# When the rows of a batch are turned: two at a time over two PSUM banks, or all four in one go over four

## What is computed

```python
# layer 0, for every batch b (x: 32 x 512 x 512, adj: 512 x 512)
y = einsum('nm,bmd->bnd', adj, x)
z = einsum('bnd,do->bno', y, weight) + bias
u = layernorm(x + z)                    # per row
# layer 1: q, k, v = u @ w_qkv ; attn = softmax(where(adj == 0, -inf, q k^T / 8))
#          o = attn v @ w_proj + b_proj ; out = layernorm(u + o + (norm(o) * gamma + beta))
```

## Time and profile before

| what | value |
|---|---|
| median of 3 runs | 3647.48 us (3646.9 to 3648.03) |
| the profiled execution: its own time | 3647.64 us |
| its span | 3645.8 us |
| TensorE (PE) busy | 3579.6 us, 98% |
| VectorE (DVE) busy | 2764.4 us, 76% |
| ScalarE (ACT) busy | 2223.4 us, 61% |
| GpSimd (POOL) busy | 1863.8 us, 51% |
| 16 DMA engines, first layer | some 55 to 65% busy, 170 to 196 GB/s |
| a batch of the first layer | 23.69 us, and 32 of them end at 777.5 us |

### The profile page before, as it was taken

The page is one execution under the profiler, slowest core; times in us unless marked ns, Lnnn a source line. Parts: engine busy times, 40 slices in busy tenths (PEclk is TensorE's granted clock), DMA queues, the critical chain, the costliest instruction groups (busy, mean ns, idle before and its releaser), DMA issues.

```text
span 3645.8 us, 64651 instructions
## 1 busy us (share of the span) xinstructions
PE 3579.6 (98%) x18960; PEld 2872.5 (79%) x18960; DVE 2764.4 (76%) x6557; ACT 2223.4 (61%) x4629; POOL 1863.8 (51%) x2559
## 2 busy tenths in 40 slices
PE   8999999999999999999999999999999999999996
PEld 6888888877777777777777777777777777777775
DVE  7666666656778787888877778787777778787787
ACT  4444443436666666666666666666666666666664
POOL 4555555532545555555555555555555555455555
PEclk9999999999999999999999999999999999999998
DMA  6555555540111111111111111111111111111111
GB/s 196 184 184 175 170 173 176 180 141 24 56 55 51 46 46 49 46 46 46 49 46 46 46 49 46 46 46 46 46 46 47 58 48 46 46 46 46 46 54 36
DMA packets 344958, 276.19 MB, mean 76 GB/s; under 512 B 13664, under 2 KB 275808, under 8 KB 344928
## 3 DMA queue, kind: packets, MB, share of 16 engines
q1 hardware_dynamic: 344928, 275.83, 24.9%
HBM read 141.56 MB, written 134.22 MB: 76 GB/s over the span
## 4 chain that ended last, share of the span: by engine, by line
PE 82%; DVE 9%; ACT 4%; issue 3%; POOL 1%; SPq 0%; DMA 0%; ACTq 0%; DVEq 0%; POOLq 0%
PE bank L813 17%; PE bank L796 10%; PE bank L829 10%; PE bank L773 10%; PE bank L311 9%; PE bank L762 9%; PE bank L324 9%; PE bank L847 6%; DVE pt_lo L1010 2%; PE bank L333 1%; ACT probs L893 1%; DVE o_stats L1036 1%; DVE ot_lo L1032 1%; DVE o L1053 1%; DVE probs L996 1%
## 5 line engine op out<-in xcount | busy, mean ns | idle before, releaser
L893 ACT ACTIVATE probs<-probs,bias_row 128x512 f32<-128x512 f32 x1024 | 729.0, 713 | 488.9 <-DVE bias_row L996 488.9
L1010 DVE TENSOR_TENSOR pt_lo<-bank,pt_hi 128x512 fp32r<-128x512 f32 x1024 | 668.2, 684 | 95.1 <-ACT pt_hi L901 82.2
L695 POOL TENSOR_SCALAR probs<-probs,inv_sums 128x480 f32<-128x480 f32 (+1 forms) x1024 | 688.3, 685 | 0.0
L996 DVE CUSTOM_DVE_ANT_0 probs<-bank,mask_bias 128x512 f32<-128x512 f32 x1024 | 661.6, 684 | 0.0
L901 ACT ACTIVATE pt_hi<-bank 128x512 fp32r<-128x512 f32 x1024 | 554.9, 594 | 132.3 <-PE bank L773 129.2
L692 POOL TENSOR_TENSOR probs<-probs,inv_sums 128x32 f32<-128x32 f32 x512 | 123.8, 242 | 986.6 <-DVE inv_sums L1002 983.0
L773 PE MATMUL bank<-ident,probs 128*128 128x128 f32 x4096 | 533.9, 273 | 20.6 <-POOL probs L695 16.9
L773 PEld LDWEIGHTS bank<-ident,probs 128*128 128x128 f32 x4096 | 477.8, 140 | 90.4 <-POOL probs L695 24.6
L813 PE MATMUL bank<-x_hi,w_hi 128*128 128x512 f32 x1024 | 411.3, 402 | 16.5 <-DVE ot L1028 6.4
L813 PE MATMUL bank<-x_hi,w_lo 128*128 128x512 f32 x1024 | 412.2, 403 | 0.0
L813 PE MATMUL bank<-x_lo,w_hi 128*128 128x512 f32 x1024 | 401.3, 392 | 0.0
(11 more groups left out here) (92 smaller groups left out, 7965.3 us busy)
## 6 DMA issues: line engine op xcount, KB each, us to landing
x_in<-in_x_dram SPq DMA_DIRECT2D x32, 1024.0 KB, 5.7
ut_hi<-ut_hi_sb SPq DMA_DIRECT2D x128, 256.0 KB, 3.5
ut_lo<-ut_lo_sb SPq DMA_DIRECT2D x128, 256.0 KB, 3.7
u_beta_rows<-ub SPq DMA_DIRECT2D x32, 1024.0 KB, 4.4
x_hi<-ut_hi SPq DMA_DIRECT2D x128, 256.0 KB, 4.3
x_lo<-ut_lo SPq DMA_DIRECT2D x128, 256.0 KB, 4.7
out_dram<-o SPq DMA_DIRECT2D x128, 256.0 KB, 3.3
ub_row<-u_beta_rows SPq DMA_DIRECT2D x124, 256.0 KB, 2.7
```

What stands on the lines that cost most here:

```text
L695: pool.tensor_scalar(probs[:, k % 2, a, cols], probs[:, k % 2, a, cols], inv_sums[:, k % 4, a:a + 1], 0.0, ALU.mult, ALU.add)\
L893: act.activation(probs[:, k % 2, a, :], probs[:, k % 2, a, :], ACT.Exp, bias=bias_row[:, k % 4, a:a + 1], scale=-1.0, accum_out=sums[:, k ...
L996: dve.tensor_tensor_reduce(probs[:, k % 2, a, :], s_bank[k % 2][a][:], mask_bias[:, k % T, :], -SCALE, 3.0e38, ALU.add, ALU.min, bias_row[ ...
L1010: dve.tensor_tensor(pt_lo[:, a, :, cols], t_bank[a][:].rearrange("p (m n) -> p m n", m=T), f32(pt_hi[:, a, :, cols]), ALU.subtract).then_i ...
```

## The change

- The turned rows get four PSUM banks (4 to 7) in place of two; in the last batch still two (4 and 5), since the second layer starts in banks 6 and 7.
- TensorE turns all four row groups of batch b - 1 in one go, behind y(b, 1). `turn(b, j)` of the same batch, between and behind the z units, is gone. The last batch's rows 0 and 1 are turned behind the loop, ahead of the first q matmuls. Batch 1 stands written out ahead of TensorE's loop.
- ScalarE's and VectorE's four `ut` parts of batch b - 1 stand behind the second y part of batch b.
- SyncE's queue stores all four turned row groups of batch b - 1 behind the store of `ub` of b - 1.

```diff
-            turn_bank = psum[4:6]
+            def turn_bank(b, j):
+                return psum[4 + (j % 2 if isinstance(b, int) and b == B - 1 else j)]
...
                     if not first:
                         store_ub(b - 1)
-                        store_ut(b - 1, 2)
-                        store_ut(b - 1, 3)
+                        for j in range(T):
+                            store_ut(b - 1, j)
                     if isinstance(b, int) and b < 2:
                         more_w(4 + 8 * b)
                     if last:
...
                         load_u_turned(sp, 0)
-                    store_ut(b, 0)
-                    store_ut(b, 1)
                     if isinstance(b, int) and b == 0:
                         more_w(8)
...
-                def turn(b, j, free=True):
-                    pe.wait_ge(u_made, b * 4 + (j + 1))
-                    if free:
-                        pe.wait_ge(utlo_made, b * 4 + (j - 1))
-                    for d in range(T):
-                        last = pe.transpose(turn_bank[j % 2][:, d * P:(d + 1) * P], u[:, j, d * P:(d + 1) * P],
-                                            ident[:])
-                    last.then_inc(u_turned, 1)
+                def turn(b):
+                    for j in range(T):
+                        pe.wait_ge(u_made, b * 4 + (j + 1))
+                        if not (isinstance(b, int) and b == 0):
+                            pe.wait_ge(utlo_made, b * 4 + (j - 3))
+                        for d in range(T):
+                            last = pe.transpose(turn_bank(b, j)[:, d * P:(d + 1) * P],
+                                                u[:, j, d * P:(d + 1) * P], ident[:])
+                        last.then_inc(u_turned, 1)
 
                 def batch(b, first=False):
                     y(b, 0, first)
-                    if not first:
-                        turn(b - 1, 2)
                     y(b, 1, first)
                     if not first:
-                        turn(b - 1, 3)
+                        turn(b - 1)
                     y(b, 2, first)
                     y(b, 3, first)
-                    z(b, 0)
-                    z(b, 1)
-                    z(b, 2)
-                    turn(b, 0, free=not first)
-                    z(b, 3)
-                    turn(b, 1, free=not first)
+                    for j in range(T):
+                        z(b, j)
 
                 batch(0, first=True)
-                with pe.Fori(1, B, 1) as b:
+                batch(1)
+                with pe.Fori(2, B, 1) as b:
                     batch(b)
...
                     for j in range(T):
                         y_hi_part(b, j)
                         w_hi_part(b, j)
-                        if not first and j < 2:
-                            ut_hi_part(b - 1, j + 2)
+                        if not first and j == 1:
+                            for turned in range(T):
+                                ut_hi_part(b - 1, turned)
...
                     normalise(b, 1)
-                    ut_hi_part(b, 0)
                     w_hi_part(b, 5)
                     normalise(b, 2)
-                    ut_hi_part(b, 1)
...
                     row_stats(b, 2)
-                    ut_lo_part(b, 0)
                     row_shift(b, 2)
                     w_lo_part(b, 5)
                     row_stats(b, 3)
-                    ut_lo_part(b, 1)
                     row_shift(b, 3)
...
+                last_turn(pe, 0)
+                last_turn(pe, 1)
                 qk_matmuls(0, 0, 12, begin=True)
                 last_turn(pe, 2)
```

More of the change, by code:

```diff
@@ L260, in _ @@
                 store_ub(B - 1)
-                store_ut(B - 1, 2)
-                store_ut(B - 1, 3)
+                for j in range(T):
+                    store_ut(B - 1, j)
                 sp.wait_ge(ub_stored, 16 * B)
@@ L360, in last_turn @@
                 for d in range(T):
-                    last = pe.transpose(turn_bank[j % 2][:, d * P:(d + 1) * P], u[:, j, d * P:(d + 1) * P],
+                    last = pe.transpose(turn_bank(B - 1, j)[:, d * P:(d + 1) * P], u[:, j, d * P:(d + 1) * P],
                                         ident[:])
@@ L385, in ut_hi_part @@
                     act.activation(ut_hi[:, :, j * P:(j + 1) * P],
-                                   turn_bank[j % 2][:].rearrange("p (d n) -> p d n", d=T), ACT.Copy)\
+                                   turn_bank(b, j)[:].rearrange("p (d n) -> p d n", d=T), ACT.Copy)\
                         .then_inc(uthi_made, 1)
@@ L429, in _ @@
                 batch(B - 1, last=True)
-                ut_hi_part(B - 1, 2)
-                ut_hi_part(B - 1, 3)
+                for j in range(T):
+                    ut_hi_part(B - 1, j)
             @block.vector
@@ L468, in ut_lo_part @@
                     cols = slice(j * P, (j + 1) * P)
-                    dve.tensor_tensor(ut_lo[:, :, cols], turn_bank[j % 2][:].rearrange("p (d n) -> p d n", d=T),
+                    dve.tensor_tensor(ut_lo[:, :, cols], turn_bank(b, j)[:].rearrange("p (d n) -> p d n", d=T),
                                       f32(ut_hi[:, :, cols]), ALU.subtract).then_inc(utlo_made, 1)
@@ L488, in batch @@
                         w_lo_part(b, j)
-                        if not first and j < 2:
-                            ut_lo_part(b - 1, j + 2)
+                        if not first and j == 1:
+                            for turned in range(T):
+                                ut_lo_part(b - 1, turned)
                     if not last:
@@ L520, in _ @@
                 batch(B - 1, last=True)
-                ut_lo_part(B - 1, 2)
-                ut_lo_part(B - 1, 3)
+                for j in range(T):
+                    ut_lo_part(B - 1, j)
         with ExitStack() as second:
```

## The result

The changed kernel takes 3653.96 us (median of 20 runs, 3650.04 to 3655.61), the kernel before 3647.26 (20 runs): a ratio of 1.0016, 95% interval 1.001 to 1.0023. By the medians that is 6.7 us more, by the ratio 5.8, against 6.8 forecast, and within the 0.2%. The profiled execution has a span of 3651.1 us against 3645.8, 5.3 more.

What follows compares the result with a forecast made beforehand. It took TensorE's own instruction stream to bound the steady state, and transfers to count at the start and where the layers meet. Terms: -3.8 + 3.2 + 1.7 + 4.3 + 1.4 = +6.8 us, so 3654.3 us, range 3646.5 to 3661.

Steps and rivals of the forecast that it cites:

- step 1: Steady batches: four turns in one go save 0.13 us per batch, 3.8 us in all (1.5 to 6).
- The cover named there: Steady batches: y units, turns and free banks hide ScalarE's and VectorE's four turned parts, so TensorE does not wait.
- step 2: Batches 0 and 1: more stores ahead of the projection weights make the last u late, 3.2 us more (2.2 to 4.7).
- the chain behind it has no slack: Batches 0 and 1: however late the first projection weight tile is, TensorE is late, through ScalarE and VectorE.
- Clock at the start: Behind TensorE's stop in batch 1: a stretch of 3.4 us at half clock, 1.7 us more (0 to 3.4).
- step 3: Where the layers meet: one more MB of stores ahead of the second layer's input, 4.3 us more (3.5 to 5.2).
- Clock at the junction: At TensorE's restart where the layers meet: half clock, net 1.4 us more (0 to 3.4).
- the clock does not fall with runs of 16 or of 32: Rival, steady batches: 16 transposes in a row bring half clock in every batch, 51 us more, 3705 us; chance 0.04.
- The stretches at half clock behind the two stops: Rival, start and junction: stretches of 6.8 us, costing 3.4 us each; +10.5 in all, 3658 us; chance 0.10.
- The weights did not come in time: Rival, batches 0 and 1: weights arrive in time and the start's loss falls away, 3648 to 3650 us; chance 0.12.
- Joining was worth 0.17 and not 0.5: Rival, steady batches: joining gives back 0.5 us per batch, 15 us in all, 3640 us; chance 0.04.

Runs made afterwards that it cites:

- One join: Kernel before, with only the turns of rows 2 and 3 of the last batch put together behind y 1: 3645.54 us, ratio 0.9995.
- two banks: Changed kernel with two PSUM banks for the turned rows in place of four: 3708.03 us, ratio 1.0165.
- input first: Changed kernel; in the last batch, SyncE's queue loads batch 0's turned rows ahead of the stores of batch 30's: 3643.64 us, ratio 0.9994.
- filler: Changed kernel with 24 matmuls that nothing reads behind the turn of (31, 1), during the wait for x_lo: 3651.26 us, ratio 1.0007.
- every turn twice: Changed kernel with every turn of the loop done twice, so that 32 transposes stand in a row: 3700.61 us, ratio 1.0147.
- the orders in the kernel before: Kernel before, projection weights and second layer's input queued ahead of turned rows' stores, weight tiles 8 to 11 left in place: 3647.13 us, ratio 0.9996.
- pure delay: Kernel before with 15 matmuls that nothing reads ahead of the second layer's first batch: 3650.74 us, ratio 1.0008.
- weights first: Changed kernel; in batch 1, SyncE's queue loads the projection weights ahead of the stores of batch 0's turned rows: 3648.46 us, ratio 1.0005.
- the pairs: Kernel before, turns joined two by two (rows 2 and 3, rows 0 and 1), SyncE's program and two banks unchanged: 3728.99 us, ratio 1.0223.

## Why the prediction was right, and where it was not

The time is as forecast, 3654.0 against 3654.3, and each step has its sign. The sizes:

- **Steady batches** (step 1): -3.8 forecast, 0.13 per batch; 0.17 measured, -4.8. One join alone gave 0.07. I had shortened the three joins by 0.02 for a longer tail behind 16 transposes, which isn't there: the row for a pair in the second layer gave 0.05 each by itself, 0.15. The cover named there held: no wait of TensorE between 100 and 760 us, and two banks showed what it costs without.
- **Start** (step 2): +3.2 forecast. Counted from the first `yt_hi`, the tile is there 3.0 us later than in the kernel before, the last u 2.5 and the turn 2.5. Three other traces with the same orders at the start (input first, filler, every turn twice) have the last u 2.9 to 3.2 later. So the size was right, though issued 4.4 us late the tile landed only some 3 late; whether that is because tiles 8 and 9 had left early, no run separates. That the chain behind it has no slack was nearly right for a later tile, but wrong for an earlier one: in the kernel before ScalarE's wait of 1.84 us was covered by VectorE's chain, as the run with the orders in the kernel before shows.
- **Clock at the start**: +1.7 forecast, +1.6 measured, and nothing in the filler's trace.
- **Junction** (step 3): +4.3 forecast; between the two profiled executions the wait grew by 2.95. The working was wrong in one term, the stores: I took 1.3 us for each, but the last three in the queue left 0.9 us apart, so that eight took from 762.3 to 770.5. The first load leaves 8.92 us behind the `ub` store in each of three traces with this part of the changed kernel and 5.26 in each of three with that of the kernel before, 3.7 us for the additional MB; the loads followed at the old pace. My 4.3 us a MB averaged over 4 MB with a start and a last landing in it. The rest of the difference is the last landing, which changes from execution to execution: with the waits of 1.22 us (pure delay) and 5.59 (weights first) the growth would be 4.4. So the 4.3 is not shown to be wrong, and 2.95 is its low end. While the eight stores left, the changed kernel's trace had 290 GB/s, which is 3.6 us a MB. The Trainium skill, "DMA: Bandwidth & Descriptors", section Specifications, with some 358 GB/s, an estimated 2.9 us a MB, lies as far below that as my 4.3 above.
- **Clock at the junction**: +1.4 forecast, +1.6 measured.

The terms come to +3.8 by the first scores, not +6.8, against this trace of the kernel before, and to +5.2 against that of the pure delay, each counted from the first `yt_hi`. That the total is right all the same is partly luck. The forecast has nothing for the very end, and there the changed kernel's trace adds 1.9 us in which the longer stretch at half clock lies. The pure delay ends on the shorter stretches with its shift of 3.4 us, so the shift alone does not bring it; what does stays open. From one execution of the changed kernel to another the time follows the clock: of the 20, the three below 3652 us have a mean granted clock of 0.994, the five above 3655 us have 0.991. Against the trace of the kernel before, then, the steady batches came out 1.0 us better than forecast, the start 0.7 and the junction's wait 1.4, and 1.9 us came at the end that it did not have.

The rivals: the clock does not fall with runs of 16 or of 32 transposes. The Trainium skill, "TensorE: Matmul & The Clock Gate", Part 4: PE-mode transpose, has them not counted as busy like matmuls; with matmuls around them no run here shows a price for that. The stretches at half clock behind the two stops lost 1.6 us each, not 3.4. The weights did not come in time. Joining was worth 0.17 and not 0.5.

## What to carry to other kernels

A change that moves stores in an in-order DMA queue has to be read transfer by transfer: what stood behind them before, what stands behind them now, and who waits for that; here two orders of a few lines in that queue were worth some 4 and 8 us by the ratios, and in the pairs, whose queue was left as it was, turned parts that came later held back a load behind them and cost 80 us, while the compute that was regrouped gave 5. Give transfers that someone waits for their place ahead of those that have time. And where TensorE is the bound, count a stop at its length plus what the clock may take behind it: 1.6 us on top of 3 to 5 here, though not behind every stop. A single trace gives the size of a wait only roughly: the same program showed 1.2 and 2.5 us for one and the same wait.

## What the runs showed of the hardware

A turn of four 128 x 128 transposes costs 0.06 us less when it stands next to another (23.69, 23.62 and 23.52 us per period with none, one and three joins). Behind one and the same wait of 2.01 us the granted clock was at half for 3.4 us in 11 traces and at 1.00 in two.

The view of the chain can leave the engine that is the bound: in the changed kernel it gave GpSimd and "issue" 23% of the span while TensorE was busy for 660.00 of 660.00 us.
